# Mixture-of-experts layers around an attention layer: ScalarE copies the transposed rows ahead of the transposed hidden values in the steps of the experts

## The reference

```python
x = x + 0.5 * _L0_ffn_ref(_layernorm(x), ...)
x = x + _L0_attn_ref(_layernorm(x), ...)
x = x + 0.5 * _L0_ffn_ref(_layernorm(x), ...)

# _L0_ffn_ref: 32 experts, each token goes to the 4 with the highest scores
t = _rmsnorm(x, norm_scale)
vals, idx = jax.lax.top_k(t @ gate_w.T + gate_b, 4)
w = softmax(vals)
h1 = einsum('th,efh->tef', t, w1) + b1        # 128 -> 256 channels
glu, lin = min(h1[..., ::2], 7), clip(h1[..., 1::2], -7, 7)
h = glu * sigmoid(1.702 * glu) * (lin + 1)    # 128 channels
out = sum over the chosen experts of w * (h @ w2[e].T + b2[e])
```

## Time and profile before

| | us |
|---|---|
| median of 3 runs (lowest, highest) | 724.32 (722.59, 725.16) |
| the profiled execution, its own time | 724.03 |
| span of its instructions | 722.1 |
| TensorE matmuls busy | 531.1 (74%) |
| GpSimd busy | 505.9 (70%) |
| VectorE busy | 436.1 (60%) |
| ScalarE busy | 347.6 (48%) |

### The profile page before, as it was taken

One profiled execution on the slowest core, in us unless ns is written; L12 is line 12 of the kernel. 1 busy time (PEld: TensorE's weight loads), 2 busy tenths in 40 slices (PEclk: granted clock), 3 DMA queues, 4 the chain that ended last, 5 costly groups with the idle time before them and its releaser, 6 DMA issues. The chain is left out here.

```text
span 722.1 us, 12842 instructions
## 1 busy us (share of the span) xinstructions
PE 531.1 (74%) x3252; PEld 446.6 (62%) x3253; DVE 436.1 (60%) x1243; ACT 347.6 (48%) x752; POOL 505.9 (70%) x551
## 2 busy tenths in 40 slices
PE   6258889999899998395607864999999999934000
PEld 3153276999899998163504552699998999834000
DVE  7889223555547778378993868255564767845222
ACT  4444414666556666495607743366665666610000
POOL 3677777777527777777677777777752777777765
PEclk9557999999999999797557955999999999967555
DMA  7997115666546665222121111456655666524222
GB/s 269 391 379 290 53 53 153 197 203 202 170 145 196 204 207 154 80 55 52 48 55 52 51 56 52 138 186 208 199 173 176 199 205 203 156 80 125 66 62 57
DMA packets 56493, 108.28 MB, mean 150 GB/s; under 512 B 12576, under 2 KB 19968, under 8 KB 56320
## 3 DMA queue, kind: packets, MB, share of 16 engines
q1 hardware_dynamic: 40064, 74.13, 31.0%
q0 software_dynamic: 16384, 33.59, 16.3%
HBM read 51.00 MB, written 56.62 MB: 149 GB/s over the span
## 5 line engine op out<-in xcount | busy, mean ns | idle before, releaser
L563 POOL DMA_INDIRECT YG<-ys,row x256 | 244.9, 956 | 116.6 <-issue 75.9
L538 POOL DMA_INDIRECT xs<-U,row x256 | 250.6, 979 | 82.0 <-issue 71.0
L1306 PE MATMUL PS<-W,xT 128*128 x768 | 182.3, 380 | 0.2
L1306 PEld LDWEIGHTS PS<-W,xT 128*128 128x128 f32 x768 | 138.4, 190 | 16.1 <-issue 1.1
L1003 DVE TENSOR_SCALAR glulin<-PS 128x512 f32<-128x512 f32 x96 | 66.3, 691 | 126.7 <-PE PS L1315 84.4
L624 ACT ACTIVATE yrow<-PS 128x512 f32<-128x512 f32 x96 | 57.4, 598 | 103.2 <-PE PS L1315 103.2
L1315 PEld LDWEIGHTS PS<-W,hidT 128*128 128x128 f32 x768 | 100.8, 193 | 8.0 <-issue 3.6
L1315 PE MATMUL PS<-W,hidT 128*128 x768 | 102.9, 277 | 1.8 <-issue 1.3
L1016 DVE SCALAR_TENSOR_TENSOR hid<-glulin,swish 128x512 f32<-128x512 f32 x96 | 66.6, 694 | 15.9 <-ACT swish L629 11.2
L629 ACT ACTIVATE swish<-glulin 128x512 f32<-128x512 f32 x96 | 60.4, 630 | 30.2 <-DVE glulin L1003 25.8
L637 ACT ACTIVATE xT<-PS 128x512 f32<-128x512 f32 x96 | 56.4, 590 | 38.5 <-PE PS L1209 38.3
(11 more groups left out here) (178 smaller groups left out, 716.9 us busy)
## 6 DMA issues: line engine op xcount, KB each, us to landing
xrow<-xs SPq DMA_DIRECT2D x96, 256.0 KB
ys<-yrow SPq DMA_DIRECT2D x96, 256.0 KB
xs<-YG SPq DMA_DIRECT2D x6, 2048.0 KB, 12.5
W<-in_w12T SPq DMA_DIRECT2D x1, 6144.0 KB
xs<-U,row POOLq DMA_INDIRECT x256
YG<-ys,row POOLq DMA_INDIRECT x256
out<-X SPq DMA_DIRECT2D x7, 256.0 KB, 2.5
X<-in_x SPq DMA_DIRECT2D x4, 256.0 KB, 3.7
```

Source lines behind the costliest of these rows:

```text
L538: pool.indirect_dma_start(out=xs[c], out_offset=bass.IndirectOffsetOnAxis(ap=row[:, i:i + 1], axis=0), in_=U[:, (c * CT + t) * H:(c * CT + ...
L563: pool.indirect_dma_start(out=YG[:, t * TOPK + k, :], out_offset=None, in_=ys[c], in_offset=bass.IndirectOffsetOnAxis(ap=row[:, i:i + 1], ...
L1306: last = te.matmul(h1, xT[:, r, q * P:(q + 1) * P], W[:, bass.ds(es[q], 2 * H)], start=True, stop=True)
```

## The change

In ScalarE's `step`, the copy of the rows' transposes moves ahead of the copy of the hidden values' transposes. Nothing is added or removed; `seam` and `end` stay as they were.

```diff
                     if live(k, 2, NGF):
                         swish_of(k - 2, r)
+                    copy_rows(k, r)
                     if live(k, 3, NGF):
                         act.wait_ge(turned, k + (t0 + 1))
                         wait_count(act, multiplied, k + (m0 - 1))
                         copy_hid(k - 3, s)
-                    copy_rows(k, r)
```

## The result

| | before | with the change |
|---|---|---|
| median of 22 runs each, us (lowest, highest) | 724.66 (722.13, 726.51) | 725.69 (723.11, 728.68) |
| ratio, 95% interval | | 1.0022 [1.0014, 1.003] |
| the profiled execution, us | 724.03 | 723.11 |
| its span, us | 722.1 | 721.4 |

A forecast was written before the change was run, and what follows sets the result against it. TensorE bounds the experts, GpSimd's indirect DMAs the stretch between layers and the tail. Holds of 0.37 + 0.30 = 0.67 us on 724.03 give 724.7, put at 724.8 towards the runs' median; range 722.8 to 726.6.

The forecast's parts named there:

- Steady steps: At TensorE's hidden transposes in steady steps, the hidden copy 0.48 us later costs 0, with 0.97 us margin left.
- The case that the cover is gone: Without the two products between the hidden copy and its use by TensorE, a step could cost up to 0.48 us.
- The releaser: Group 24's hidden copy releases the first chunk's gather on GpSimd, which starts 0.48 us later in either layer; bounds 0 and 0.48.
- The rival: At the gather's start the store, not the hidden copy, releases it, so nothing moves: 724.0 us; chance 0.38.
- Lateness of the first addition: VectorE's first gathered addition, already waiting for its DMA, starts 0.48 us later; the DMA lands 0 to twice 0.48 later.
- Hold of TensorE: At step 31's hidden transposes TensorE starts 0.30 us later in the first layer and 0.37 us in the second.
- No further tiles held: Gathered tiles after the first cost nothing, as each tile gains 2 us of margin on the one before.
- the rival with 7.4 us: Each of the 10 gathered tiles in both layers lands late and holds TensorE: 7.4 us, 731.4 us in all; chance 0.07.
- Slack ahead of the next gathers: GpSimd's slack before the next gathers, 0.82 and 1.17 us, absorbs the late gather; idle time there shrinks by about 0.2 us.
- The second layer's start: The second layer's experts were to start about 0.3 us later, as a sign that the forecast is right.

The follow-up runs named there:

- chips B and C: Two slower chips, kernel before 867.64 and 872.06 us; kernels with the new copy order and other gather gates or step 27 kept old measured 1.0076 to 1.0103 there.
- the kernel with the gate back: The changed kernel, but the gather's first DMA waits for step 27's row copy instead of its hidden copy; 724.04 us, ratio to before 1.0003 [0.9994, 1.0012].

## Why the prediction was right, and where it was not

- **Steady steps: right here.** The hidden copy 0.48 us later costs TensorE nothing where the margin is 0.97 us; the kernel with the gate back shows it (1.0003). The case that the cover is gone turned up on chips B and C, and there a loss of clock came with it that the prediction did not think of.
- **The releaser: right, by a hair.** The gather follows the hidden copy by 0.86 us in both kernels. But the argument for it was wrong. The store was priced from the ends of the experts at 2.89 to 3.15 us and so put 0.88 us ahead of the copy; in the middle of the experts it takes 4.08 to 4.33 us where it is the last condition, so that it was level with the copy, or up to 0.2 us ahead. That the copy was last in before is luck as far as the argument goes. The rival named the reason, the DMA engines' load. The Trainium skill (Perfetto Trace Analysis, section DMA Instruction — HWDGE) says that the signal follows the confirmed write, with a delay that can be long. These rows agree, and show that the delay isn't the same everywhere. Had the change made the hidden copy earlier, the rival would have been the case.
- **Lateness of the first addition: the term that was too small.** The prediction took 0.48 us, "because nothing else of the gather changes". It was 0.74 and 0.63 us (column a), since the gather's second DMA moved into VectorE's `hid` and grew by 0.38 and 0.26 (0.12 and 0.11 of it do not reach the addition). The range of 0 to 0.96 us had it. The row of that DMA and of `hid`, 0.31 us apart, stood in the trace of before and was not looked at.
- **Hold of TensorE: right in place, too small.** The prediction's own step, lateness less 0.18 us in the first layer and less 0.11 in the second, would with the measured lateness give 0.56 + 0.52 = 1.08 us. The step of TensorE grew by 0.62 + 0.69 = 1.31. The rest, 0.06 and 0.17, is what TensorE loses after the wait, where the next product's loads show 0.18 and 0.29 us of idle time for no releaser. 0.67 us were forecast, 1.31 are in the trace, 1.6 (1.0 to 2.2) in the runs.
- **No further tiles held: right.** The additions have two waits, as before; the rival with 7.4 us did not come true.
- **Slack ahead of the next gathers: not to be told.** It shrank by 0.05 and 0.25 us where 0.2 had been forecast, but in the later execution of the same kernel the idle times are 1.09 and 0.47 us, and with the gate back 1.86 and 1.55: they scatter by more than 0.2. **The second layer's start** can't be read either: the first layer's seam moves it by over 1 us with the granted clock.

## What to carry to other kernels

Swapping two short operations of an engine that is not the bound is free only towards those who have margin: list every waiter for the one that comes later, above all the single events (the start of a gather) with another engine's work queued behind them. When a stream of GpSimd's DMAs is shifted by a few tenths of a us, lay it against VectorE's operations of the same step and see which DMA now starts inside one. Take the price of a store's signal from a place with the same DMA load. And before two traces are compared, compare the granted clock of their stretches.

## What was not expected of the hardware

**GpSimd's indirect DMAs and `hid`.** In the trace of before, 30 of the 512 indirect DMAs start between 0.05 and 0.6 us after the start of a `hid` (0.69 us, two operands in SBUF). Those near its start last 1.4 to 1.5 us and those near its end 0.95 to 1.0; whatever their start, all 30 end 0.81 to 0.85 us after the end of `hid`. Of the 482 others none is longer than 1.14 us. In the changed kernel it is 31, with 0.82 to 0.86 us. The same traces hold a comparison: 79 DMAs of before start in the same way inside a `glu` or `lin`, which last 0.69 us too but read PSUM, and take 0.94 to 0.96 us (76 with 0.94 to 0.98 in the changed kernel). The shorter additions of line 979 (0.34 us, two operands in SBUF) do the same as `hid`: the two DMAs that start 0.13 and 0.14 us after one take 1.03 and 1.02 us and end 0.82 us after its end. A row of it in the changed kernel, at the end of the addition's step:

```profile
221.64 0.69 DVE L1016 SCALAR_TENSOR_TENSOR hid<-glulin,swish 128x512 f32<-128x512 f32 x1 [0.20 <-ACT swish L629]
...
221.93 1.22 POOL L563 DMA_INDIRECT YG<-ys,row  x1 [0.30 <-issue]
```

It ends at 223.15, 0.82 us after 222.33. So it looks as if such a DMA does its part only once `hid` is over, while one that has started first is not slowed: in the changed kernel the five that start within 0.03 us of `hid` take 0.94 to 0.96. The traces show this as a coincidence of times, in all kernels alike; no run was made for it by itself. The Trainium skill (SBUF — State Buffer, section SBUF: two separate sides) has a rule of this kind: the port pair that VectorE and GpSimd share is a lock for a whole instruction, which a VectorE operation "with two SBUF inputs" takes, though only against a GpSimd operation that reads SBUF. The rows agree in one direction, with `glu` and `lin` free of it; the indirect DMAs take their row numbers from an array in SBUF (`row`), but that this is the read in question is not shown, and a DMA that started first is not seen to hold `hid`, which takes 0.68 to 0.73 us in all cases of before.

**The same kernel on other chips.** 724.01, 867.64 and 872.06 us for the kernel before, with a mean granted clock of TensorE of 0.81 to 0.83 in the slower executions, 0.84 in the faster: the clock does not account for 20%. On the slower chips engines other than TensorE stand idle for "remote" (87 us for `yrow` and 59 for `hidT` in one execution, none in before's table). What that is stays open.
